# A sum of relu1 at the end of VectorE's step instead of ahead of the third product, in a recommendation tower's interaction layer

## The reference

```
z = einsum('bhd,bmd->bhmd', h, x0).reshape(batch, H * M, dim)   # h = x0 = e, then h = 64 rows of layer 0
out = relu(einsum('bcd,oc->bod', z, W) + b)
# layer 0: out[:, :64] is the h of layer 1, out[:, 64:] is kept; layer 1: all 128 rows are kept
result = sum(concatenate(kept, axis=1), axis=-1)               # over the 64 of dim
y = relu(relu([result, dense_ctx] @ W_top1 + b) @ W_top2 + b) @ W_top3
```

## Time and profile before

| | us |
|---|---|
| median of three runs | 2170.9 |
| lowest and highest | 2169.59 and 2172.28 |
| the profiled execution's own time | 2169.86 |
| its span, first to last instruction | 2168.0 |
| PE busy | 2065.0 (95%) |
| DVE busy | 1785.7 (82%) |
| POOL busy | 1723.6 (79%) |
| ACT busy | 1556.8 (72%) |

### The profile page before, as it was taken

How to read it: one execution, slowest core, us unless ns; L and a number is a source line. 1 busy time by engine, 2 the same in 40 slices (tenths; PEclk the granted TensorE clock), 3 DMA queues, 4 the chain that set the end, 5 groups by cost and what they waited for, 6 DMA issues and landing times.

```text
span 2168.0 us, 27494 instructions
## 1 busy us (share of the span) xinstructions
PE 2065.0 (95%) x6856; PEld 1271.6 (59%) x6856; DVE 1785.7 (82%) x1227; ACT 1556.8 (72%) x1814; POOL 1723.6 (79%) x708
## 2 busy tenths in 40 slices
PE   3999999999999999999999999999999999999998
PEld 1565665665665665665665665665665665665663
DVE  3888888888888888888888888888888888888871
ACT  3777777777777777777777777777777777777762
POOL 3888888888888888888888888888888888888761
PEclk9999999999999999999999999999999999999999
DMA  7987876877877876876876877877877876876720
GB/s 191 215 191 163 187 171 161 188 171 162 187 171 161 188 174 158 188 170 162 189 172 160 187 170 162 188 172 161 187 172 161 187 174 160 187 174 159 185 53 0
DMA packets 268303, 364.11 MB, mean 168 GB/s; under 512 B 107505, under 2 KB 107889, under 8 KB 268162
## 3 DMA queue, kind: packets, MB, share of 16 engines
q1 hardware_dynamic: 258338, 352.61, 71.5%
q0 software_dynamic: 8192, 8.40, 1.5%
q10 hardware_dynamic: 1760, 2.96, 0.5%
HBM read 347.02 MB, written 16.78 MB: 168 GB/s over the span
## 4 chain that ended last, share of the span: by engine, by line
PE 62%; DVE 20%; issue 11%; ACT 4%; DVEq 1%; SPq 1%; DMA 1%; POOL 1%; ACTq 0%
PE out L622 48%; PE out L613 12%; DVE prod L559 10%; DVE prod L564 7%; ACT relu L379 4%; DVE z L561 2%; DVE feat L523 1%; POOL zl L218 0%; SPq L260 0%; PE out L671 0%; DMA fields_dram<-emb 0%; PE hrep L671 0%; DVEq L523 0%; SPq L285 0%; SPq L270 0%
## 5 line engine op out<-in xcount | busy, mean ns | idle before, releaser
L218 POOL TENSOR_TENSOR zl<-prod,zh 128x2048 fp32r<-128x2048 f32 (+1 forms) x384 | 1469.5, 3843 | 271.4 <-ACT zh L373 220.9
L373 ACT ACTIVATE zh<-prod 128x2048 fp32r<-128x2048 f32 (+1 forms) x384 | 624.3, 1626 | 199.3 <-DVE prod L559 158.8
L622 PE MATMUL out<-zh,w1h 128*128 128x512 f32 x1536 | 651.0, 424 | 4.3 <-POOL zl L218 4.3
L622 PE MATMUL out<-zl,w1h 128*128 128x512 f32 x1536 | 599.1, 390 | 0.0
L622 PE MATMUL out<-zh,w1l 128*128 128x512 f32 x1536 | 597.9, 389 | 0.0
L613 PE MATMUL out<-prod,w_sb 128*128 128x512 f32 x1024 | 508.9, 620 | 57.7 <-DVE prod L564 35.1
L386 ACT ACTIVATE hrep<-out,b_sb 32x512 f32<-32x512 f32 (+1 forms) x768 | 494.1, 643 | 15.1 <-PE out L608 5.3
L606 PE MATMUL out<-prod,w_sb 128*128 128x512 f32 x1024 | 465.2, 597 | 35.6 <-DVE prod L495 30.7
L613 PEld LDWEIGHTS out<-prod,w_sb 128*128 128x128 f32 x1024 | 174.1, 189 | 367.0 <-DVE prod L564 140.5
L622 PEld LDWEIGHTS out<-zh,w1h 128*128 128x128 f32 x1536 | 288.5, 188 | 91.6 <-issue 30.5
L622 PEld LDWEIGHTS out<-zh,w1l 128*128 128x128 f32 x1536 | 288.7, 188 | 86.9 <-issue 30.4
(11 more groups left out here) (52 smaller groups left out, 862.3 us busy)
## 6 DMA issues: line engine op xcount, KB each, us to landing
rot_low<-fields_dram SPq DMA_DIRECT2D x512, 256.0 KB
rot_high<-fields_dram SPq DMA_DIRECT2D x512, 256.0 KB
xrep<-fields_dram SPq DMA_DIRECT2D x256, 128.0 KB
fields_dram<-emb SPq DMA_DIRECT2D x512, 32.0 KB
left_x<-fields_dram SPq DMA_DIRECT2D x256, 64.0 KB, 3.8
left_y<-fields_dram SPq DMA_DIRECT2D x256, 64.0 KB, 2.3
emb<-in_tables,idx POOLq DMA_INDIRECT x256
w_sb<-in_w ACTq DMA_DIRECT2D x1, 1024.0 KB
```

The source lines that it names most:

```text
L218: pool.tensor_tensor(zl[u][:, :, :], product[:, 0:SIZES[u], :], zh[u][:, :, :].bitcast(F32), ALU.subtract).then_inc(zl_made[u], 1)
L373: act.activation(zh[u][:, :, :], product, ACT.Copy).then_inc(zh_made[u], 1)
L622: mm = nc.tensor.matmul(out1[:, :], w[:, k, :], z[:, t, :], start=False, stop=stop and t == SIZES[u] - 1 and part == 2)
```

## The change

`sum_l1(m - 1)` stood between `prod[2]` and `prod[3]` in DVE's step m. Now it is the last thing of the step, behind prod4. The instruction and its wait for `relu1_made` are the same. One wait is new: z4 now waits for `zl_made[3]` of the step before, which DVE itself counts up when the instruction that reads z4 is done. ACT, PE, POOL and SP have the same instructions in the same order.

```
                nc.vector.tensor_tensor(prod[2][:, :, :], repeated(hrep[0], LOW), high[:, :, :],
                                        ALU.mult).then_inc(p2_made, 1)
-                if later:
-                    sum_l1(m - 1)
                dve.wait_ge(hrep1_made, m + 1)
                if later:
                    dve.wait_ge(zl_made[2], m)
                    dve.wait_ge(whole3_used, m)
                nc.vector.tensor_tensor(prod[3][:, :, :], repeated(hrep[1], LOW), high[:, :, :],
                                        ALU.mult).then_inc(p3_made, 1)
+                if later:
+                    dve.wait_ge(zl_made[3], m)
                nc.vector.tensor_tensor(z4[:, :, :], repeated(hrep[1], 2), low[:, 0:2, :], ALU.mult).then_inc(z4_made, 1)
                if later:
                    dve.wait_ge(whole4_used, m)
                nc.vector.tensor_tensor(prod4[:, :, :], repeated(hrep[1], 2), low[:, 2:4, :],
                                        ALU.mult).then_inc(p4_made, 1)
+                if later:
+                    sum_l1(m - 1)
```

## The result

The changed kernel takes **2044.66 us** (median; 2043.91 to 2045.08 in four runs) against 2171.56 us before on the same chip: a ratio of 0.9417, 95% interval 0.940 to 0.9433. The forecast was 2045, between 2034 and 2060. The profiled execution took 2043.91 us with a span of 2042.1.

What follows compares the result with a forecast made beforehand. A once-a-step ring through PE, ACT and DVE was taken as the bound, PE's own pace afterwards. Span 2168.0 - 123.5 - 4.3 = 2040.2 led to 2043 us; between that and 2047 it predicted 2045, range 2034 to 2060.

Steps and rivals of the forecast that it cites:

- The ring and what closes it: Split matmuls, relu1, sum, third product, z4, prod4, `whole` circle once a step, 16.30 us; DVE's sum holds the third product.
- PE's pace from its weight loads: PE without waits takes 15.28 us a step against 16.26, gaining 0.98 in each of 126 steps, 123.5 us.
- The sum by mean steps: Span 2168.0 less 123.5 for the steps and 4.3 at the end, plus execution differences, gives 2043 us.
- the pace of 15.22: PE's step time assumed for the range's lower bound: with the whole gain at the end it gives 2034 us.
- The rule weighed: Whether PE's busy time or its weight loads show the gain to be had: 2113 us by busy row, 2045 by loads.
- The rival that went by the busy rows: Only the idle time shown in the busy rows can be won: 2113 us, chance 0.03.
- What is late next: Other engines in an odd step: smallest spare 1.9 us, for DVE's prod4 ahead of PE's need; nothing waits.
- T: The moment when PE's split matmuls of step m-1 are done; relu1 is there at T + 0.7.
- Nearest rival: POOL's 14.62 us step, 0.66 below 15.28, or another ring takes over first: 2060 to 2110 us, chance 0.06.
- The new wait of z4: z4 on DVE waits for zl_made[3]: bounds 0 and 0.1 us a step, taken as 0.
- The end: In step 127 PE's shorter pause saves 2.95 us, `whole` at full clock 1.7, less 0.3 for POOL's zl: 4.3.
- The clock rival: With PE never pausing its granted clock falls and the kernel is slower, about 2190 us at 15%; chance 0.02.

Runs made afterwards that it cites:

- Runs 1: Changed kernel with DVE's third product waiting for relu1_made again, the sum staying at the step's end: 2081.02 us, ratio 0.9589 to the kernel before.
- run 9: Changed kernel plus two idle 128x1024 products on DVE per step, one operand in PSUM, directly ahead of the third product: 2150.23 us, ratio 0.9906 to the kernel before.
- run 6: Changed kernel plus one idle 128x512 sum on POOL behind the third low part of each step: 2079.18 us, ratio 0.9577 to the kernel before.
- run 4: Changed kernel plus one idle 128x1024 product on DVE per step, both operands in SBUF, ahead of the third product: 2466.58 us, ratio 1.1368 to the kernel before.
- run 5: Changed kernel plus two idle 128x1024 products on DVE per step, both operands in SBUF, ahead of the third product: 2868.15 us, ratio 1.3197 to the kernel before.
- run 3: Changed kernel with the sum and its wait placed between the third product and z4: 2045.18 us, ratio 0.9424 to the kernel before.
- run 2: Changed kernel with the sum back ahead of the third product, summing relu1 of two steps past from two buffers: 2044.25 us, ratio 0.942 to the kernel before.
- runs 7: Changed kernel with the third product's third tile split for PE, DVE making its low part at the next step's start: 2037.78 us, ratio 0.9382 to the kernel before.
- 10: Changed kernel with the third product's third tile split, its low part on DVE behind prod[1] of the next step: 2025.48 us, ratio 0.9336 to the kernel before.
- run 8: Changed kernel plus one idle 128x1024 product on DVE per step, one operand in PSUM, directly ahead of the third product: 2045.47 us, ratio 0.9426 to the kernel before.

## Why the prediction was right, point by point

- **The ring and what closes it.** Right. Runs 1 and 2 show both halves: with the wait alone put back, 36 us of the 126 return; with the sum put back and no wait, nothing does. The rest of the 126, some 90 us (0.71 a step), comes from taking the sum with its register instruction from behind that wait.
- **PE's pace from its weight loads.** 15.28 predicted, 15.30 measured. The stretch of 36 loads is 1012.51 - 1004.10 = 8.41 here, where the one step in the earlier trace rows had 8.39. That is 2.5 us less gain than the 123.5 worked out.
- **The forecast of 2045.** The mechanism was right; that the number is right to 0.3 us is partly luck. The sum by mean steps came to 2043. The 2047 that was averaged with it rests on a single step (0.95 us instead of 0.98), and happened to make up for the 2.5 us. Of the bounds, no row gives the pace of 15.22 or the 0.1 us a step for the new wait.
- **The rule weighed.** The rival that went by the busy rows gave 2113 and is wrong by 68 us. PE's busy time fell from 2065.0 to 1996.7 although it does the same instructions: 68 us of what was counted as busy was waiting. The Trainium skill's page Perfetto Trace Analysis, Identifying the Most-Contended Engine, which calls matmul busy time no good measure, is borne out. The page's reason is that pipelined instructions look smaller in the trace; here they looked longer, because a waiting matmul counted as busy.
- **What is late next.** No waits in the middle of the run, as forecast. The third product was over at T + 1.2 rather than T + 0.8, and prod4 at T + 3.5 rather than 3.1; a first part was line 505, which idled 0.36 us in odd steps. The spare to PE's need at T + 5.0 was 1.5 us, not 1.9. The prediction used this spare only to say that nothing waits, and for that it was good. As a measure of the room for more work it is the wrong one: run 9 shows that the mean work of DVE decides, which leaves 1.4 us. The prediction also had the sum covered by line 495's wait for layer 0, and in the odd step shown it was not quite: line 495 started at T + 4.0, where layer 0 was done at T + 3.7. It cost nothing, since line 512 still waited 0.62 us for ACT.
- **POOL.** Nearest rival, as said, with 1.1 us of mean room (run 6).
- **The new wait of z4.** Taken as 0. The page of the kernel after has z4 with no idle time ahead of it, and the sum of the parts leaves nothing over.
- **The end.** 4.3 predicted, 4.3 measured. PE pauses 0.87 us instead of 3.70 and takes 3.67 for the eight `whole` instructions instead of 5.41, and its 36 split matmuls take 0.2 longer than before, about what was set down for POOL's zl (0.3):

```profile
1992.96 3.67 PE L615 MATMUL out<-prod,w_sb 128*128 128x512 f32 x8 [0.87 <-ACT relu L379]
```

```profile
1994.00:2006.00 12.00, 11.07 (x43) 7.53 (x41) 2.27 (x4) 4.42 (x6) 6.93 (x2) 1.00 0.00 0
```

  The second row is the windows view behind the pause (us, busy of PE, PEld, DVE, ACT, POOL, then the clock): 1.00, where it was 0.61.
- **The clock rival.** The granted clock stayed at full with PE at 98% (0.998 in the mean). The means that lie clearly lower belong to the runs in which PE was busy least, 0.959 in run 4 (87%) and 0.89 in run 5 (77%).

## What to carry to other kernels

A short instruction that waits for the end of the bounding engine's work, placed ahead of that engine's next input, costs the wait, its own length and its issue, once for every turn. Move it behind the products that the other engine wants (behind the first of them was enough, run 3), or give its input a second buffer (run 2); both gave the whole gain here. To see what such a move is worth, take the bounding engine's pace from the starts of its weight loads and not from its busy share, and check the other engines' mean work a step against that pace. Work that is added on DVE fits into such room only if nothing holds it up: an instruction of 1.21 us took 4.79 in the median beside POOL's subtractions (run 4).

## What the runs showed of the hardware that I had not expected

A DVE `tensor_tensor` with both operands in SBUF and a POOL `tensor_tensor` keep each other waiting. The 128x1024 product took 1.21 us when it had started ahead of POOL's instruction and 5.58 us when it started 0.09 us behind one of 4.58 us (run 4). Where two of POOL's instructions followed each other without a pause it could be held through both, 9.45 us in all (the longest in run 4). The 128x512 low part took 0.68 or up to 5.41 us (runs 7 and 10). POOL is held up too: its subtractions took 4007 ns in the mean in run 7 against 3856 after the change. With one operand in PSUM the same 128x1024 product took 1208 to 1220 ns in all 128 steps, beside a subtraction of POOL in 125 of them (run 8):

```profile
L559 DVE TENSOR_TENSOR spent<-hrep,rot_low x128: 1208/1215/1220, 44.0 to 1990.7; 128x1024 f32<-128x1024 f32 x128
```

DVE's sums with a single SBUF operand (line 523) are not touched either: 0.67 to 0.69 us after the change, nearly all of them beside a subtraction. The Trainium skill's GPSIMD Engine Reference, Key points, says that POOL shares its SBUF interfaces with VectorE and names two SBUF inputs as a case of contention; the trace agrees, and adds that a DVE instruction can be held for the whole of a POOL instruction. The kernel escapes this because every product and subtraction of DVE in its loop reads one operand from PSUM (`xr`, `hrep`, `lz` or `z4`); line 501, for one, took 0.69 us in each of its 64 instances, 63 of them beside a subtraction of POOL.
